# A four-layer graph network kernel: first product in halves, the passage from layer one to layer two reordered

## The reference

```
h = relu(layernorm(x));  x = x + L0(h)   # adj.T * (q k^T), rows divided by their norm, times v
h = relu(layernorm(x));  x = x + L1(h)   # graph attention: leaky relu scores, mask, softmax, elu
h = relu(layernorm(x));  x = x + L2(h)   # normalised adjacency times (h W), bias
h = relu(layernorm(x));  x = x + L3(h)   # 8-head attention with q, k, v, output projections
```

## Time and profile before

| what | value |
|---|---|
| median of 3 runs | 711.36 us (711.34 to 711.44) |
| profiled execution | 711.51 us |
| its span, first to last instruction | 709.7 us |
| PE / PEld busy | 692.0 us (98%) / 653.5 us (92%) |
| DVE / ACT / POOL busy | 597.7 (84%) / 582.5 (82%) / 460.7 (65%) |
| chain that ended last | PE 88%, ACT 3%, DVE 3%, issue 2%, POOL 1%, DMA 1% |
| granted TensorE clock | 1.000 |

### The profile page before, as it was taken

How to read it: one execution, slowest core, us unless ns; L and a number is a source line. 1 busy time by engine, 2 the same in 40 slices (tenths; PEclk the granted TensorE clock), 3 DMA queues, 4 the chain that set the end, 5 groups by cost and what they waited for, 6 DMA issues and landing times.

```text
span 709.7 us, 22689 instructions
## 1 busy us (share of the span) xinstructions
PE 692.0 (98%) x6950; PEld 653.5 (92%) x6950; DVE 597.7 (84%) x2523; ACT 582.5 (82%) x2020; POOL 460.7 (65%) x581
## 2 busy tenths in 40 slices
PE   8999999999999999999998999999999999999996
PEld 7999999998788888889997999999999999999994
DVE  6998988886588888699998889888888888888876
ACT  3787777777799999877765998889888988898895
POOL 2455656473378677589884766776677667766762
PEclk9999999999999999999999999999999999999999
DMA  8222310000000000000000000000000000000001
GB/s 249 91 90 90 90 28 0 0 0 1 1 2 1 2 1 2 1 2 0 0 0 2 17 32 17 30 30 30 15 30 30 30 15 30 30 30 16 32 32 45
DMA packets 21708, 20.29 MB, mean 29 GB/s; under 512 B 2448, under 2 KB 21648, under 8 KB 21648
## 3 DMA queue, kind: packets, MB, share of 16 engines
q1 hardware_dynamic: 19456, 18.16, 8.1%
q10 hardware_dynamic: 2192, 1.44, 0.7%
HBM read 11.21 MB, written 8.39 MB: 28 GB/s over the span
## 4 chain that ended last, share of the span: by engine, by line
PE 88%; ACT 3%; DVE 3%; issue 2%; POOL 1%; DMA 1%; POOLq 0%; ACTq 0%; DVEq 0%
PE bank L410 43%; PE bank L1293 8%; PE bank L400 7%; PE bank L172 5%; PE bank L1279 5%; PE bank L1303 4%; PE bank L494 4%; PE bank L856 3%; PE bank L441 3%; PE bank L390 3%; PE bank L475 1%; PE bank L894 1%; PE bank L869 1%; ACT prob L1389 1%; DVE stats L135 1%
## 5 line engine op out<-in xcount | busy, mean ns | idle before, releaser
L1389 ACT ACTIVATE prob<-wide,small 128x128 f32<-128x128 f32 x504 | 195.6, 393 | 2.1 <-DVE small L1501 2.1
L1464 POOL TENSOR_TENSOR prob<-prob,small 128x512 f32<-128x512 f32 x127 | 132.4, 1043 | 98.7 <-DVE small L1515 96.7
L1501 DVE CUSTOM_DVE_ANT_0 wide<-bank,mbias 128x128 f32<-128x128 f32 x512 | 115.1, 285 | 0.5 <-issue 0.5
L1389 ACT ACTIVATION_READ_ACCUMULATOR prob<-wide,small 128x1 f32 x504 | 96.1, 191 | 0.0
L1293 PE MATMUL bank<-ident,prob 128*128 128x128 f32 x512 | 72.3, 273 | 3.8 <-POOL prob L1464 3.5
L161 POOL TENSOR_TENSOR rstd<-vare,mhalf 128x2 f32<-128x2 f32 x88 | 61.7, 702 | 16.6 <-DVE vare L150 16.3
L659 POOL TENSOR_TENSOR rnorm<-norm,mhalf 128x2 f32<-128x2 f32 x32 | 22.3, 697 | 74.0 <-ACT relsq L594 74.0
L247 POOL TENSOR_SCALAR xn<-xs,nmean,rstd 128x256 f32<-128x256 f32 x120 | 65.8, 559 | 5.5 <-POOL rstd L161 5.5
L135 DVE BATCH_NORM_STATS2 stats<-xs 128x6 f32<-128x256 f32 (+1 forms) x176 | 65.5, 414 | 4.2 <-DMA xs<-in_x_dram 3.2
L1409 ACT COPY probT<-bank 128x512 f32<-128x512 f32 x96 | 52.0, 576 | 17.9 <-PE bank L1293 17.9
L1293 PEld LDWEIGHTS bank<-ident,prob 128*128 128x128 f32 x512 | 58.2, 140 | 5.5 <-POOL prob L1464 4.5
(11 more groups left out here) (176 smaller groups left out, 1949.7 us busy)
## 6 DMA issues: line engine op xcount, KB each, us to landing
out_dram<-xs SPq DMA_DIRECT2D x31, 256.0 KB, 2.1
xs<-in_x_dram SPq DMA_DIRECT2D x29, 256.0 KB, 2.7
xs<-in_x_dram ACTq DMA_DIRECT2D x1, 512.0 KB, 8.3
xs<-in_x_dram ACTq DMA_DIRECT2D x1, 256.0 KB, 3.7
wq<-in_L_gnn_Wq_dram SPq DMA_DIRECT2D x1, 256.0 KB, 3.4
wk<-in_L_gnn_Wk_dram ACTq DMA_DIRECT2D x1, 256.0 KB, 4.7
wv<-in_L_gnn_Wv_dram SPq DMA_DIRECT2D x1, 256.0 KB, 5.8
w<-in_L_gnn_W_dram SPq DMA_DIRECT2D x1, 256.0 KB, 7.2
```

What stands on the lines that cost most here:

```text
L1389: ins = nc.scalar.activation(prob[:, r, i, :], wide[:, r, i, :], ACT.Exp, bias=nmax[r][:, i:i + 1], scale=-1.0, accum_out=rsum[r][:, i:i + 1])
L1464: nc.gpsimd.tensor_tensor(prob[:, r, :, :], prob[:, r, :, :], rinv[r].unsqueeze(2).to_broadcast([128, QUAD, N]), ALU.mult).then_inc(prob_r ...
L1501: nc.vector.tensor_tensor_reduce(out=wide[:, r, i, :], in0=SS[r][:, i * N:(i + 1) * N], in1=mbias[:, :], scale=-1.0, scalar=3e38, op0=ALU. ...
```

## The change

Four things are changed.

1. **The query-key product in halves.** Each half goes to a bank of its own (`MM` and `RR`), the first transposes stand between the two halves, and ScalarE's and VectorE's copies are split in the same way. `t_product(0)` now also waits for the second low half (`m_low`).
2. **The end of layer one.** The first transposes of layer two move ahead of `relation(31)`. On ScalarE `copy_v(31)` comes first, then layer two's first activations, `relation_high(31)`, `squares(31)`, and only then the sums and squares of pair 29. On VectorE `low_v(31)` moves ahead of `update(30)`.
3. **Layer two's first products in two bank pairs.** `product(1)` and `product(3)` go to banks 6 and 7, the others to 1 and 2. For p below 4 a product waits only for the copy of the product two before. The order on TensorE in the first steps is written out anew.
4. **The last odd moments.** The sums of pair 31 move from ScalarE's step 2 to step 1; the squares stay in step 2. `root_odd` moves from GpSimd's step 11 to step 3.

```diff
+        query_key_bank = [MM, RR]
...
-                for d in range(C):
+                def query_key(d):
                     for e in range(C):
-                        ins = nc.tensor.matmul(MM[:, d * D:(d + 1) * D], wq0[:, e, d * 128:(d + 1) * 128],
+                        ins = nc.tensor.matmul(query_key_bank[d][:, 0:D], wq0[:, e, d * 128:(d + 1) * 128],
                                                wk0[:, e, :], start=(e == 0), stop=(e == C - 1))
-                ins.then_inc(m_done, 1)
+                    ins.then_inc(m_done, 1)
+
+                query_key(0)
                 pe.wait_ge(c_ident, 1)
                 pe.wait_ge(xn_ready, 1)
                 transposes(HT).then_inc(tr_done, 1)
+                query_key(1)
                 pe.wait_ge(wv_loaded, 16)
                 turn_weight(WV, wv0)
+                pe.wait_ge(m_low, 1)
                 t_product(0, 0)
...
                 values(PAIRS - 1, 1)
+                pe.wait_ge(l1_xn_ready, 1)
+                pe.wait_ge(hT_ready, PAIRS)
+                transposes(HT).then_inc(l1_tr_done, 1)
                 relation(PAIRS - 1, 1)
                 relation_outputs(PAIRS - 2)
                 turn_relation(PAIRS - 1, 1)
-                pe.wait_ge(l1_xn_ready, 1)
-                transposes(HT).then_inc(l1_tr_done, 1)
...
                 squares(PAIRS - 2, 0)
+                copy_v(PAIRS - 1)
+                act.wait_ge(l1_tr_done, 1)
+                act.wait_ge(rel_done, PAIRS - 1)
+                nc.scalar.activation(hT_flat, HT[:, :], ACT.Relu).then_inc(l1_hT_ready, 1)
+                relation_high(PAIRS - 1)
+                squares(PAIRS - 1, 1)
                 sums_odd(act, PAIRS // 2 - 2)
                 squares_odd(act, PAIRS // 2 - 2)
-                copy_v(PAIRS - 1)
-                relation_high(PAIRS - 1)
-                act.wait_ge(l1_tr_done, 1)
-                act.wait_ge(rel_done, PAIRS)
-                nc.scalar.activation(hT_flat, HT[:, :], ACT.Relu).then_inc(l1_hT_ready, 1)
-                squares(PAIRS - 1, 1)
...
-                dve.wait_ge(c_high, 1)
-                nc.vector.tensor_tensor(m_qk[1][:, :, :], as_chunks(MM), m_qk[0][:, :, :].bitcast(F32), ALU.subtract)
+                def query_key_low(d):
+                    dve.wait_ge(c_high, d + 1)
+                    return nc.vector.tensor_tensor(m_qk[1][:, d, :], query_key_bank[d][:, 0:D], m_qk[0][:, d, :].bitcast(F32),
+                                                   ALU.subtract)
+
+                query_key_low(0)
                 low_part(0, 0)
+                query_key_low(1).then_inc(m_low, 1)
                 normalise(1)
...
+                    if p + 1 == PAIRS:
+                        low_v(p)
                     update(p - 1)
-                    low_v(p)
+                    if p + 1 < PAIRS:
+                        low_v(p)
...
+            def product_banks(p):
+
+                return banks[:, 6:8, :] if p in (1, 3) else banks[:, 1:3, :]
...
-                    pe.wait_ge(val_ready, since(p))
-                    for g in range(2):
-                        ins = node_product(HG[:, g, 0:D + 2], w1, g)
+                    pe.wait_ge(val_ready, since(p - 1 if p < 4 else p))
+                    for g in range(2):
+                        ins = node_product(product_banks(p)[:, g, 0:D + 2], w1, g)
...
                 for p in range(PAIRS - 1):
                     step(p)
+                    if p == 1:
+                        sums_odd(act, PAIRS // 2 - 1)
                     if p == 2:
-                        sums_odd(act, PAIRS // 2 - 1)
                         squares_odd(act, PAIRS // 2 - 1)
...
-                    if p == 11:
+                    if p == 3:
                         root_odd(pool, PAIRS // 8 - 1)
```

More of the change, by code:

```diff
@@ L201, in gnn_stack_kernel @@
         raw_loaded = [sem(f"c_raw_loaded{k}") for k in range(5)]
-        c_plain = sem("c_plain")
+        c_plain, m_low = sem("c_plain"), sem("c_m_low")
         c_zeros, c_ident, c_mhalf = sem("c_zeros"), sem("c_ident"), sem("c_mhalf")
@@ L609, in _, with query_key_high @@
                     act.dma_start(bk[:, :], w["L3_gnn_bk"].rearrange("(c p) -> p c", p=128)).then_inc(rows_loaded, 16)
-                act.wait_ge(m_done, 1)
-                nc.scalar.copy(m_qk[0][:, :, :], as_chunks(MM)).then_inc(c_high, 1)
+                def query_key_high(d):
+                    act.wait_ge(m_done, d + 1)
+                    nc.scalar.copy(m_qk[0][:, d, :], query_key_bank[d][:, 0:D]).then_inc(c_high, 1)
+                query_key_high(0)
                 act.wait_ge(tr_done, 1)
                 nc.scalar.activation(hT_high, HT[:, :], ACT.Relu).then_inc(high_ready, 1)
+                query_key_high(1)
                 act.wait_ge(turned, 1)
@@ L781, in _ @@
                 statistics(1, 1)
-                dve.wait_ge(c_high, 1)
-                nc.vector.tensor_tensor(m_qk[1][:, :, :], as_chunks(MM), m_qk[0][:, :, :].bitcast(F32), ALU.subtract)
+                def query_key_low(d):
[3 more added lines that the diff above has]
+                query_key_low(0)
                 low_part(0, 0)
+                query_key_low(1).then_inc(m_low, 1)
                 normalise(1)
                 degrees()
-                dve.wait_ge(c_high, 2)
+                dve.wait_ge(c_high, 3)
                 nc.vector.tensor_tensor(wv0T[1][:, :, :], as_chunks(WV), wv0T[0][:, :, :].bitcast(F32),
@@ L846, in gnn_stack_kernel @@
             stats_ready, rstd_ready = l1_stats_ready, l1_rstd_ready
-            HT, HG, PT, EE, UU = bank[0], banks[:, 1:3, :], bank[3], bank[4], bank[5:8]
+            HT, PT, EE, UU = bank[0], bank[3], bank[4], bank[5:8]
+            def product_banks(p):
+                return banks[:, 6:8, :] if p in (1, 3) else banks[:, 1:3, :]
             nmax_b, rsum_b, rinv = [small[:, 0:2], small[:, 8:10]], [small[:, 2:4], small[:, 6:8]], small[:, 4:6]
@@ L916, in _ @@
                 spread(0)
-                for p in range(1, PAIRS):
+                product(1)
+                turn(2)
+                product(2)
+                spread(1)
+                turn(3)
+                product(3)
+                spread(2)
+                turn_prob(0)
+                turn(4)
+                attend(0)
+                spread(3)
+                turn_prob(1)
+                for p in range(4, PAIRS):
                     step(p)
@@ L926, in copy_h @@
                     act.wait_ge(att_done, since(p - 3))
-                    nc.scalar.copy(valb[p % 4][:, :, :], HG[:, :, 0:D + 2]).then_inc(val_ready, 1)
+                    nc.scalar.copy(valb[p % 4][:, :, :], product_banks(p)[:, :, 0:D + 2]).then_inc(val_ready, 1)
                 def copy_pT(p):
```

## The result

The changed kernel takes 712.49 us (median of 20 runs, 712.38 at the least) against 711.58 us for the kernel before (median of 20, 711.29 at the least). The ratio is 1.0014 with a 95% interval of 1.0009 to 1.002: some 0.9 us slower, inside the 0.2% that was called no change. The profiled execution took 712.42 us with a span of 710.6, against 711.51 and 709.7. The forecast was +0.79 us and 712.1.

A forecast was written before the change was run, and what follows sets the result against it. Layer one was taken as bound by TensorE, so edits pay only where it idles, nearly 5 us of 711. Terms 0.07 + 0.27 + 0.20 + 0.16 + 0.11 + 0.49 - 0.51 = +0.79 us give 712.1 us, range 710.9 to 712.9.

The forecast's parts named there:

- the passage: From layer one to two: transposes ahead of outputs(30) delay copy_v(31), low_v(31) and product(0), +0.27 us (-0.2 to +0.44).
- the first steps: Layer two's first products: +0.20 us to product(1), 0 to product(2), +0.16 to product(3), +0.11 to product(4).
- the odd roots: Leaving step 11 gives -0.51 us; in step 3 they wait for pair 31's squares, making turn(5) late, +0.49 (0.11 to 1.2).
- the start: First query-key product in halves: t_product(0) needs the second low half too and starts later, +0.07 us, all of it staying.
- The moments in front of copy_h(0): ScalarE's sums and squares of pair 29 now precede copy_h(0), making it and product(1) late, +0.20 us (0 to +0.35).
- The bank pairs: Product(1) to product(2): they remove the wait for copy_h(1), but single-buffered hT still ends last, 0 us.
- rival A: Bank pairs work: products 2 and 3 start 2.28 us apart instead of 3.21; total -1.8 us, 709.6; chance 0.08.
- The order: TensorE's first steps: turn(3) behind spread(1) costs product(3) +0.16 us; late spread(1) and attend(0)'s wait cost product(4) +0.11 (-0.4 to +0.6).
- VectorE decides. It enters at 8.81: Step of the start term: VectorE, taken as never idle before its first subtraction, sets the first large product's time; +0.07 us.
- everything between and behind them is carried along unchanged: Outside the start, passage, first steps and product 13 stall nothing changes, 0 us; the last 500 us shift as one block.

The follow-up runs named there:

- Run 3: The kernel before with only the second part, the reordered end of layer one; 712.19 us against 711.79, ratio 1.0008.
- run 11: The changed kernel with layer two's first transposes back behind turn_relation(31), ScalarE's and VectorE's new orders kept; 712.33 us against 711.65 for the kernel before.
- Run 5: The changed kernel with both bank pairs kept but TensorE's old order of the first steps; 711.31 us against 711.52 for the kernel before, ratio 0.9999.
- run 9: Kernel before with start halves, early sums, roots in step 4, two hT buffers, both bank pairs, new orders on TensorE and ScalarE; 709.85 us against 711.65.
- run 10: Two activation buffers and new order, but every product in banks 1 and 2, waiting for the copy before; 711.56 us against 711.65 for the kernel before.
- run 1: The kernel before with only the third part, bank pairs and TensorE's new order of the first steps; 713.15 us against 711.79, ratio 1.0018.
- run 2: The kernel before with only the fourth part, pair 31's sums in step 1 and odd roots in step 3; 710.44 us against 711.79, ratio 0.9985.
- run 4: The changed kernel with its third part undone, one bank pair and TensorE's old order; 711.18 us against 711.79 for the kernel before, ratio 0.9995.
- run 7: The kernel before with only the first part, the query-key product in halves; 711.98 us against 711.52, ratio 1.0006.
- run 6: The changed kernel with the odd roots back in GpSimd's step 11, pair 31's sums still in step 1; 712.40 us against 711.52 for the kernel before.

## Why the prediction was right

The sum was +0.79 us; the trace gives +0.89 at the last large product and the medians +0.91. The mechanism was right at the passage, in the first steps and at the odd roots. That the total is off by only 0.10 us is in part luck: the start was 0.14 us better than forecast, and the odd roots and layer three were 0.09 and 0.13 worse. Point by point:

- **The passage** came as worked out. copy_v(31) was forecast for 175.36 and started at 175.32, low_v for 176.00 and started at 175.94, product(0) for 176.89 and started at 176.84. Run 3 shows this part by itself, run 11 that the transposes ahead of outputs(30) are its cause.
- **The moments in front of copy_h(0)**: forecast at 179.15 and product(1) at 180.30, found at 179.08 and 180.19. Its own line, 177.30 + 1.94, gives 179.24 and not the 179.15 that it goes on with.
- **The bank pairs** bring nothing, and for the reason given: one `hT`. Run 5 shows the banks neutral, runs 9 and 10 that they work once the buffer is doubled and the order fits. That was rival A's mechanism; its products 2.28 us apart are what run 9 has with 2.18. It needed an edit that the change did not make.
- **The order**: +0.16 and +0.11 were forecast for products 3 and 4, +0.17 and +0.12 found. But the price of the order is larger than these two terms, for +0.11 is what is left of two effects. From product(3) to product(4) it was 4.33 us before; the order alone makes it 5.39 (run 1), the early sums alone 3.59 (run 2), and both together 4.45. The prediction weighed them in one term, and so didn't see that the change without the order would have been a gain. Undone, the order gives 1.08 us at product(4) and 0.24 more at turn(5) (run 4). The term's own lines are also looser than its value. TensorE's pieces and a wait of some 0.4 us make 3.12 us from product(3) to attend(0), against 2.93 before, so +0.19; it was 3.04, as the wait was 0.16.
- **The odd roots**: +0.49 forecast, +0.58 found; GpSimd took 1.49 us for pair 5, as the earlier trace rows had it, and turn(5) waited. VectorE's attention beside it was slowed too, 0.84 for 0.61 us. The Trainium skill, page SBUF — State Buffer, section "SBUF: two separate sides", says that of a VectorE instruction with two SBUF inputs and a GpSimd instruction that reads SBUF, the one that starts first shuts the other out until it is through. The trace agrees in kind, since both were slowed. It doesn't show so strict a lock: GpSimd's 1.09 us of work, VectorE's leaky of 0.43 and its attention of 0.61 fitted into 1.49 us.

**Two terms were wrong.** The start was forecast at +0.07 and came at -0.07. The step that failed was "VectorE decides. It enters at 8.81". It was read from the missing bracket in the earlier trace rows, which says only that the idle time was too short to be listed. In the kernel before, VectorE's last statistics began at 8.64 us, and ScalarE's copy of the whole product was done only at 8.78:

```profile
8.19 0.59 ACT L611 CAST m_qk<-bank 128x512 fp32r<-128x512 f32 x1 [0.97 <-PE bank L519]
...
8.64 0.15 DVE L150 SCALAR_TENSOR_TENSOR vare<-mv 128x2 f32<-128x2 f32 x1
```

With the half, and in run 3 with the whole copy done earlier, the subtraction starts 0.07 us behind the start of the statistics, and here 0.17 behind. So it waited 0.10 us for the copy. The price of the extra instruction was right, 0.06 us for the 0.07 forecast (run 7), and is just paid from that. Of the 0.14 us between forecast and trace, the other 0.04 are the profiled execution's own: its first normalisation began at 6.75 us, against 6.79 before.

Second, "everything between and behind them is carried along unchanged" does not hold to a tenth: 0.13 us came in layer three, bit by bit after 325 us, and the prediction had named this as a sign of being wrong. It is not one execution's chance, and seems to go with the early odd roots. From product(13) to the last large product it is 483.00 to 483.08 us in the four full-clock profiles that have the roots in step 11, and 483.14 to 483.23 in the seven that have them early. Its cause was not tried.

## What to carry to other kernels

A loop can be held by two resources, here a result bank and an operand buffer. Doubling the bank alone gained nothing; look which wait ends last after the first is gone, and double both. Then look what the sooner work runs into: of 2.32 us gained at product(3), 0.6 were left in the time (run 9). Before moving work ahead of an idle time, see who is queued behind it: the transposes and the moments were moved out of waits that cost nothing, into places in front of work that was waited for. Filler work, like moments and roots, belongs in the first step in which its inputs are long done and nobody waits for that engine's next result; one step too early cost 0.2 to 0.6 us here.

## What the runs showed of the hardware

TensorE's granted clock can fall near the end of the program. The profiled execution of run 6 took 713.52 us with a span of 711.7, 1.1 us more than the changed kernel's, though its product(13) is only 0.08 us behind. Its stretches near the end, with the columns of the earlier trace rows:

```profile
698.00:700.00 2.00, 0.74 (x5) 0.51 (x6) 0.80 (x3) 2.00 (x9) 1.86 (x2) 1.00 0.29 97
700.00:702.00 2.00, 1.53 (x10) 1.32 (x11) 1.97 (x5) 1.42 (x5) 0.22 (x1) 0.89 0.14 42
702.00:704.00 2.00, 2.00 (x12) 2.00 (x11) 1.74 (x4) 0.00 (x0) 0.82 (x1) 0.50 0.00 0
704.00:706.00 2.00, 1.33 (x14) 1.00 (x16) 0.25 (x1) 1.17 (x2) 0.00 (x0) 0.76 0.32 108
```

TensorE had been busy for 0.74 us of the first 2, waiting for the last heads' softmax, and then had 0.50 for some microseconds, that is 1.2 of 2.4 GHz. The same twelve matmuls took 2.48 us there and 1.66 in the changed kernel's profile, where it had been busy for 0.78 of the same 2 us and kept the full clock. So behind nearly the same gap the clock sometimes falls and sometimes doesn't, and where it falls 1 us is lost. The same kernel shows both: 5 of the changed kernel's 20 executions had a mean clock of 0.997 or 0.998 and took 713.52 to 713.60 us, the other 15 had 0.999 or 1.000 and took at most 712.77. None of the 20 executions of the kernel before beside them had such a clock. All comparisons by the numbered products above end long before it.
